# The second attention's exponentials in units of three heads instead of pairs

## The chip, the cores and the metric

The kernel runs on one core of one Trainium2 chip. The metric is the device time of one execution in microseconds; a kernel's time is the median over its runs. The core has four computing engines that run their own instruction streams and meet at semaphores: TensorE (PE in the profile, with PEld for its weight loads), VectorE (DVE), ScalarE (ACT) and GpSimd (POOL). SyncE (SP) issues the transfers. TensorE writes its results into eight banks of PSUM, each 512 fp32 columns wide on 128 partitions; ScalarE and VectorE read them there and write SBUF.

## The reference, cut to what matters

Two post-norm transformer layers over x of shape (4, 2048, 256), each an attention and a feed-forward part. Only the second layer's attention is touched:

```python
H, HD = 16, 16
q, k, v = (x @ Wq.T, x @ Wk.T, x @ Wv.T)      # reshaped to (B, S, H, HD)
q, k = _rope(q, k)
scores = jnp.einsum('bqhd,bkhd->bhqk', q, k) / np.sqrt(HD)
scores = jnp.where(causal, -jnp.inf, scores)
attn = jax.nn.softmax(scores, axis=-1)
out = jnp.einsum('bhqk,bkhd->bqhd', attn, v).reshape(B, S, 256)
return out @ Wo.T
```

## The kernel before

The program is a sequence of phases: set-up, projections of layer 0, its attention, its feed-forward part, then the same for layer 1. `attend_phase(nc, kn, layer)` builds both attentions; the branches with `layer == 1` are the second one.

**Tiling.** Scores are computed transposed, 128 keys on the partitions by 512 queries (TG) in the columns, one PSUM bank for one head. Four heads (HQ) are worked on together. A *step* S is one such tile for four heads; on the diagonal `even_steps` puts two pieces of narrower width side by side, so that every step is 512 columns wide. A set is one batch and one quad of heads: 34 steps (NST), in four query groups with 2, 7, 10 and 15 steps in order of their arrival. There are 16 sets, so N = 544 steps and 2176 heads of scores.

**Per step in the second attention.** PE multiplies keys by queries (L739, bf16, one matmul of 512 columns per head, two or more narrower ones on diagonal steps) into banks 0 to 5. ScalarE takes the exponential (L805) from PSUM into `prob`, a ring of R = 4 steps in SBUF. On masked steps VectorE sets entries above the diagonal to zero with a minimum (L844, `diagonal`). PE multiplies `prob` by the values, with a column of ones for the sum (L768, `weigh`; fp32, two matmul records per head in the profile, the four heads in four strips of 32 rows of one bank), adding up over the steps of a query group in bank 6 or 7. At the end of a group VectorE transposes, divides and transposes again (`normalise`), and SP stores.

**Pairs.** Scores are made by `scores(S, pair)`, two heads at a time, into one of three pairs of banks. The pair's index is 2S + pair. Before it writes, PE waits for exponential number 2S + pair - 3 (L731), the last reader of these banks. ScalarE runs 1088 exponentials of two heads, 1024 columns each; each waits for its scores (`qk`) and for the weighing of step S - 4, whose place in `prob` it overwrites (`pv`, L804).

**Order on PE.** It is written out by hand. In the second attention each turn S of the loop at L773 issues `scores(S + 1, 0)`, `weigh(S - 2)`, `scores(S + 1, 1)`. Between two weighings thus stand the second pair of one step and the first pair of the next.

**Order elsewhere.** ScalarE goes through the pairs in order. VectorE masks step S where it must and then does the normalising that is due, which waits for the weighing (`pv`) of the group's last step. SP loads *stacks* (keys, queries, values of one query group, 14 transfers each); queries are in a ring of three (QU), so the load of group n waits for the first transpose of group n - 3 (`o_tr`). PE waits for a stack at the group's first step (L729).

`Count` numbers the events of one semaphore; `c.wait(eng, n)` returns once event n has happened, and for a negative n at once.

Of the kernel before, what the change touches and what calls it, by code (L numbers as in the profile page):

```python
# [20 lines left out]
ACT = mybir.ActivationFunctionType  # L21
# [4 lines left out]
H, HD = 16, 16  # L26
P = 128
DC = D // P
TG = 512
GB = T // TG  # L30
TT = TG // P
KB = T // P
CB = TG // P
HQ = 4
# [590 lines left out]
def attend_phase(nc, kn, layer):  # L625
# [9 lines left out]
    N = N_SET * NST  # L635
    NG = N_SET * GB
    ND = sum(1 for _, m in steps if m)
    R = 4
    LAG = 2
    QU, KU = 3, 6  # L640
    QK0, E0, O0 = 0, 4, 6
    SR, FR = (QROWS, FROWS + 3) if layer == 0 else (QROWS + 3, 0)
    with ExitStack() as ctx:
# [3 lines left out]
        qk = ph.count("qk")  # L647
# [71 lines left out]
        @block.tensor  # L719
        def _(pe):  # L720
            for c in (qk, ex, pv):
                c.start(pe)
            pe.wait_ge(ones_in, 16)

            def scores(S, pair):
                it, _, pieces, _ = at(S)
                if pieces[0][1] == 0 and pair == 0:
                    n = it * GB + pieces[0][0]
                    pe.wait_ge(stacks_in[n % QU], (n // QU + 1) * (16 * N_LOAD))  # L729
                if layer == 1:  # L730
                    pr.wait(pe, 2 * S + pair - 3)  # L731
                elif pair == 0:
                    th.wait(pe, S - 1)
                for h in (2 * pair, 2 * pair + 1):
                    bank = QK0 + (h if layer == 0 else 2 * ((2 * S + pair) % 3) + h % 2)
                    for g, kb, q0, col, w in pieces:
                        n, c = it * GB + g, it * GB + kb // CB
                        keys = k_s[:, c % KU, h, (kb % CB) * P:(kb % CB + 1) * P]
                        mm = pe.matmul(ps[:, bank, col:col + w], keys, q_s[:, n % QU, h, q0:q0 + w], start=True, stop=True)  # L739
                if layer == 1 or pair == 1:  # L740
                    qk.done(mm)

            def extra(S, h):
                it, _, pieces, masked = at(S)

                sc.wait(pe, S * HQ + h - 2)
                for g, kb, q0, col, w in pieces:
                    n, c = it * GB + g, it * GB + kb // CB
                    mm = pe.matmul(ps[:, E0 + h % 2, col:col + w], g_s[:, c % KU, (kb % CB) * P:(kb % CB + 1) * P], f_s[:, n % QU, h, q0:q0 + w], start=True, stop=not masked)  # L749
                    if masked:  # L750
                        mm = pe.matmul(ps[:, E0 + h % 2, col:col + P], kn["identb"][:], kn["mask_kq"][:], start=False, stop=True)  # L751
                ex.done(mm)

            def weigh(S):
                it, s, pieces, masked = at(S)
                if layer == 0:
                    pr.wait(pe, S)
                elif masked:
                    kept.wait(pe, (it * ND + kept_at[s]) * 2 + 1)
                else:  # L760
                    pr.wait(pe, S * 2 + 1)
                for g, kb, q0, col, w in pieces:
                    n, c = it * GB + g, it * GB + kb // CB
                    if kb == 0:

                        o_tr.wait(pe, n - 2)
                    for h in range(HQ):
                        mm = pe.matmul(ps[VW * h:VW * (h + 1), O0 + n % 2, q0:q0 + w], v_s[:, c % KU, kb % CB, h * VW:(h + 1) * VW], prob[:, S % R, h, col:col + w], start=kb == 0, stop=g in ends[s] and (g, kb) == [p[:2] for p in pieces if p[0] == g][-1])  # L768
                pv.done(mm)

            scores(0, 0)
            scores(0, 1)
            for S in range(N + LAG):  # L773
                if layer == 1 and S + 1 < N:
                    scores(S + 1, 0)
                if S >= LAG:
                    weigh(S - LAG)
                if layer == 0 and S < N:
                    extra(S, 0)
                    extra(S, 1)  # L780
                    if S + 1 < N:
                        scores(S + 1, 0)
                if S + 1 < N:
                    scores(S + 1, 1)
                if layer == 0 and S < N:
                    extra(S, 2)
                    extra(S, 3)

        @block.scalar
        def _(act):  # L790
            for c in (th, pr):
                c.start(act)

            for S in range(N + 1):
                if S < N:
                    if layer == 0:
                        qk.wait(act, S)
                        sc.wait(act, (S - 2) * HQ + HQ - 1)
                        th.done(act.activation(tanh_s[:, S % 2], ps[:, QK0:QK0 + HQ], ACT.Tanh, scale=kn["rbeta"][:, 0:1]))  # L799
                    else:  # L800
                        for pair in range(2):
                            qk.wait(act, S * 2 + pair)
                            bank = QK0 + 2 * ((2 * S + pair) % 3)
                            pv.wait(act, S - R)  # L804
                            pr.done(act.activation(prob[:, S % R, 2 * pair:2 * pair + 2], ps[:, bank:bank + 2], ACT.Exp, scale=float(HD) ** -0.5))  # L805
                if S > 0 and layer == 0:
                    sc.wait(act, (S - 1) * HQ + HQ - 1)
                    pr.done(act.activation(prob[:, (S - 1) % R], prob[:, (S - 1) % R], ACT.Exp))  # L808

        @block.vector  # L810
        def _(dve):
            for c in (sc, o_tr, o_rc, o_mul, o_n, kept):
                c.start(dve)
            dve.memset(oq_s[:], 0.0).then_inc(padded, 1)
            dve.wait_ge(padded, 1)

            def normalise(due, count):

                for S, G, part in due[:count]:
                    v = G % 2  # L820
                    if part == 0:
                        pv.wait(dve, S)
                        o_mul.wait(dve, G - 2)
                        o_tr.done(dve.transpose(ot_s[:, v].rearrange("p b n -> p (b n)"), ps[:, O0 + v]))  # L824
                    elif part == 1:
                        o_tr.wait(dve, G)
                        o_rc.done(dve.reciprocal(rc_s[:, v], ot_s[:, v, :, HD]))
                    elif part == 2:
                        o_rc.wait(dve, G)
                        o_n.wait(dve, G - 2)  # L830
                        o_mul.done(dve.tensor_tensor(oq_s[:, v, :, 0:HD], ot_s[:, v, :, 0:HD], rc_s[:, v].unsqueeze(2).to_broadcast([P, NTB, HD]), ALU.mult))
                    else:
                        o_mul.wait(dve, G)
                        o_out.wait(dve, v, G // 2 - 1)
                        o_n.done(dve.transpose(on_s[:, v], oq_s[:, v].rearrange("p b n -> p (b n)")))
                del due[:count]

            def diagonal(S):

                masked = at(S)[3]  # L840
                for pair in range(2):
                    pr.wait(dve, S * 2 + pair)
                    block = blocks(prob[:, S % R, 2 * pair:2 * pair + 2], masked)
                    kept.done(dve.tensor_tensor(block, block, kn["keep"][:].unsqueeze(1).unsqueeze(1).to_broadcast([P, 2, len(masked), P]), ALU.min))  # L844

            def sums(S, due):

                pv.wait(dve, S - R)
                for h in range(HQ):
                    if h == 2:  # L850

                        normalise(due, 1)
                    th.wait(dve, S)
                    ex.wait(dve, S * HQ + h)
                    sc.done(dve.scalar_tensor_tensor(prob[:, S % R, h], tanh_s[:, S % 2, h], kn["alpha"][:, 0:1],  # L855
                                                     ps[:, E0 + h % 2], ALU.mult, ALU.add))

            due = []
            for S in range(N + LAG + 1):
                if S > LAG:  # L860
                    it, s, *_ = at(S - LAG - 1)
                    due += [(S - LAG - 1, it * GB + g, part) for g in ends[s] for part in range(4)]
                if S < N and layer == 0:
                    sums(S, due)
                else:
                    if S < N and at(S)[3]:
                        diagonal(S)
                    normalise(due, len(due))
            assert not due
# [711 lines left out]
```

## Time and profile before

| | |
|---|---|
| median of 3 runs | 4268.65 us (4263.97 to 4272.33) |
| profiled execution | 4269.56 us, span 4267.4 us |
| PE, PEld busy | 3718.8 us (87%), 1427.9 us (33%) |
| ACT, DVE busy | 3382.7 us (79%), 2744.3 us (64%) |
| second attention | first exponential at 2864.5 us, last at 3946.3 us |
| its exponentials (L805) | 1088, 1054.9 us busy, mean 1021 ns |
| mean granted TensorE clock | 0.968 of full speed |

The page gives the busy time of each engine as a share of the whole span, and the whole span has six stages with different limits. The stage to read is the second attention, about 1083 us from its first exponential to the end of its last. Two engines are nearly always busy in it. The rows further down cut the span by stretch, by line and in order of time. Names in rows: `ps` is PSUM, `att_q`, `att_k`, `att_v` and `att_prob` are the phase's tiles, `att_v<-v_ones` is the last transfer of a stack, and numbers like 128x1024 are partitions by columns. PE's records overlap, because a matmul is recorded until its last result has left the array, so the start of one to the start of the next is what a matmul costs.

### The profile page before, as it was taken

How to read it: one execution, taken by the hardware profiler on the slowest of the kernel's cores; microseconds unless marked ns; L12 is line 12 of the kernel's file. 1: busy time of each engine (PE TensorE's matmuls, PEld its weight loads, DVE VectorE, ACT ScalarE, POOL GpSimd, SP SyncE). 2: the span in 40 equal slices, each digit the busy share in tenths (PEclk: the TensorE clock that was granted, in tenths of full speed). 3: DMA queues.
4: the chain of work that ended last, by engine and by line, in shares of the span. 5: the costliest groups of instructions: out<-in, count | busy, mean ns of one | idle time of the engine just before them, and what ended most of it. 6: DMA issues, size and time to landing. Idle time of an engine off the chain costs nothing. (4 is left out here: it accounts for less than half of the span.)

```text
span 4267.4 us, 65356 instructions
## 1 busy us (share of the span) xinstructions
PE 3718.8 (87%) x21966; PEld 1427.9 (33%) x21966; DVE 2744.3 (64%) x4748; ACT 3382.7 (79%) x2760; POOL 450.1 (11%) x407
## 2 busy tenths in 40 slices
PE   6968989998998998899897857749999999999787
PEld 2422323222332322233232644422222222222565
DVE  5637887778888777888876978853323233232688
ACT  2428999999999999999998113339999999999233
POOL 3530000000000000000000216630000000000232
PEclk9979999999999999999999989879999999999899
DMA  5862111112111111211111545652222222221333
GB/s 168 260 200 57 52 53 45 46 50 60 52 53 52 45 45 51 60 51 54 52 45 45 147 146 159 195 149 69 71 76 72 65 79 68 76 73 48 110 89 89
DMA packets 307803, 360.37 MB, mean 84 GB/s; under 512 B 56590, under 2 KB 237934, under 8 KB 307249
## 3 DMA queue, kind: packets, MB, share of 16 engines
q1 hardware_dynamic: 307508, 356.62, 28.9%
q8 instruction: 163, 2.67, 0.3%
q14 instruction: 132, 1.08, 0.1%
HBM read 228.15 MB, written 128.25 MB: 84 GB/s over the span
## 5 line engine op out<-in xcount | busy, mean ns | idle before, releaser
L855 DVE SCALAR_TENSOR_TENSOR att_prob<-att_tanh,alpha,ps 128x512 f32<-128x512 f32 x2176 | 1507.2, 741 | 431.0 <-ACT att_tanh L799 371.1
L739 PE MATMUL ps<-att_q,att_k 99*128 99x512 bf16 (+5 forms) x5120 | 1136.7, 351 | 159.9 <-DMA att_v<-v_ones 104.0
L768 PE MATMUL ps<-att_prob,att_v 128*32 128x512 f32 (+3 forms) x10240 | 1161.8, 539 | 2.2 <-ACT att_prob L808 2.2
L799 ACT ACTIVATE att_tanh<-ps,rbeta 128x2048 f32<-128x2048 f32 x544 | 1110.6, 2042 | 59.8 <-PE ps L739 59.7
L805 ACT ACTIVATE att_prob<-ps 128x1024 f32<-128x1024 f32 x1088 | 1054.9, 1021 | 38.7 <-PE ps L739 22.9
L808 ACT ACTIVATE att_prob<-att_prob 128x2048 f32<-128x2048 f32 x544 | 1081.2, 1988 | 1.7 <-DVE att_prob L855 1.3
L749 PE MATMUL ps<-att_f,att_g 75*128 75x512 bf16 (+3 forms) x2560 | 810.4, 354 | 131.3 <-DVE att_prob L855 121.2
L739 PEld LDWEIGHTS ps<-att_q,att_k 96*128 96x128 bf16 (+1 forms) x5120 | 399.9, 98 | 1007.7 <-ACT att_prob L805 424.8
L844 DVE TENSOR_TENSOR att_prob<-att_prob,keep 128x512 f32<-128x512 f32 (+1 forms) x320 | 187.5, 586 | 587.9 <-ACT att_prob L805 586.8
L749 PEld LDWEIGHTS ps<-att_f,att_g 75*128 75x128 bf16 x2560 | 231.9, 96 | 922.1 <-DVE att_prob L855 899.5
L768 PEld LDWEIGHTS ps<-att_prob,att_v 128*32 128x32 f32 x10240 | 216.0, 108 | 347.9 <-ACT att_prob L805 139.0
L1233 POOL TENSOR_TENSOR post_x1b<-post_x,post_bias 128x256 f32<-128x256 f32 x64 | 46.6, 757 | 2193.3 <-DVE post_x L1042 2193.3
L404 POOL TENSOR_TENSOR proj_parts<-proj_rem,proj_parts 128x512 bf16<-128x512 f32 (+2 forms) x176 | 224.7, 1279 | 136.9 <-DVE proj_parts L564 97.9
L1031 ACT ACTIVATE post_n_sd<-post_n_mv,eps 128x4 f32<-128x4 f32 x64 | 18.9, 295 | 249.7 <-DVE post_n_mv L1026 249.7
L751 PE MATMUL ps<-mask_kq,identb 128*128 128x128 bf16 x1024 | 211.1, 221 | 0.0
L824 DVE STREAM_TRANSPOSE att_ot<-ps 128x512 f32<-128x512 f32 x128 | 91.2, 712 | 185.1 <-PE ps L768 185.1
L1458 POOL TENSOR_SCALAR post_prev<-post_xt,post_om 128x512 f32<-128x512 f32 x64 | 56.8, 905 | 1188.9 <-issue 1146.4
L564 DVE CAST proj_parts<-proj_rem 128x512 bf16<-128x512 f32 (+2 forms) x176 | 152.6, 871 | 0.0
L421 ACT ACTIVATE proj_vs<-ps 128x512 f32<-128x512 f32 x64 | 38.2, 597 | 136.2 <-PE ps L516 96.8
L1042 DVE TENSOR_SCALAR post_x<-post_rr,post_n_rs,post_n_nb 128x256 f32<-128x256 f32 x256 | 122.1, 539 | 7.4 <-DVE post_n_nb L1037 0.2
L508 PE MATMUL ps<-proj_xt,proj_wq 128*128 128x512 f32 x256 | 125.7, 637 | 0.8 <-ACT proj_xt L430 0.8
L516 PE MATMUL ps<-proj_wv,proj_xt 128*128 128x256 f32 x512 | 123.5, 384 | 1.8 <-ACT proj_vs L421 1.5
(132 smaller groups left out, 2462.4 us busy)
## 6 DMA issues: line engine op xcount, KB each, us to landing
att_k<-k_parts SPq DMA_DIRECT2D x768, 64.0 KB
att_q<-q_parts SPq DMA_DIRECT2D x768, 64.0 KB
v_ones<-proj_vs SPq DMA_DIRECT2D x128, 256.0 KB, 3.1
att_v<-v_ones SPq DMA_DIRECT2D x128, 256.0 KB
post_o<-o_t SPq DMA_DIRECT2D x40, 512.0 KB, 5.1
att_f<-f_parts SPq DMA_DIRECT2D x384, 48.0 KB
o_t<-att_on SPq DMA_DIRECT2D x512, 32.0 KB, 1.9
q_parts<-proj_parts SPq DMA_DIRECT2D x32, 384.0 KB, 4.2
```

What stands on the lines that cost most here:

```text
L404: low.done(pool.tensor_tensor(parts[0:n, rp, 2], rem[0:n, r], parts[0:n, rp, 1], ALU.subtract))
L508: mm = pe.matmul(ps[0:n, PRJ0 + r], lhs, xt[:, u, c], start=c == 0, stop=c == DC - 1)
L564: mid.done(dve.tensor_copy(parts[0:n, (s - L_MID) % RP, 1], rem[0:n, r]))
L739: mm = pe.matmul(ps[:, bank, col:col + w], keys, q_s[:, n % QU, h, q0:q0 + w], start=True, stop=True)
L749: mm = pe.matmul(ps[:, E0 + h % 2, col:col + w], g_s[:, c % KU, (kb % CB) * P:(kb % CB + 1) * P], f_s[:, n % QU, h, q0:q0 + w], start=True ...
L751: mm = pe.matmul(ps[:, E0 + h % 2, col:col + P], kn["identb"][:], kn["mask_kq"][:], start=False, stop=True)
L768: mm = pe.matmul(ps[VW * h:VW * (h + 1), O0 + n % 2, q0:q0 + w], v_s[:, c % KU, kb % CB, h * VW:(h + 1) * VW], prob[:, S % R, h, col:col + ...
L799: th.done(act.activation(tanh_s[:, S % 2], ps[:, QK0:QK0 + HQ], ACT.Tanh, scale=kn["rbeta"][:, 0:1]))
L805: pr.done(act.activation(prob[:, S % R, 2 * pair:2 * pair + 2], ps[:, bank:bank + 2], ACT.Exp, scale=float(HD) ** -0.5))
L808: pr.done(act.activation(prob[:, (S - 1) % R], prob[:, (S - 1) % R], ACT.Exp))
L844: kept.done(dve.tensor_tensor(block, block, kn["keep"][:].unsqueeze(1).unsqueeze(1).to_broadcast([P, 2, len(masked), P]), ALU.min))
L855: sc.done(dve.scalar_tensor_tensor(prob[:, S % R, h], tanh_s[:, S % 2, h], kn["alpha"][:, 0:1], ps[:, E0 + h % 2], ALU.mult, ALU.add))
```

## The change

In the second attention the heads of all steps form one stream, numbered 4S + h. A *unit* is three heads of this stream. There are 726 units, of which the last has one head. Unit u writes banks 0 to 2 or 3 to 5 in turn, waits for exponential u - 2, and is read by one exponential of 1536 columns, which writes three neighbouring places in `prob`, now a ring of six steps. A step's last head lies in unit (4S + 3) // 3; the weighing of the step is issued after the unit three further on. Units cross the borders of steps, groups and sets. The masks wait for the unit that holds their heads. In the first attention the issue order stays: its two pairs of scores were already next to each other. The code of both is separated.

```diff
-    R = 4
+    R = 4 if layer == 0 else 6
...
+    UH = 3
+    NU = -(-N * HQ // UH)
...
+            def score(S, h, bank):
                 it, _, pieces, _ = at(S)
-                if pieces[0][1] == 0 and pair == 0:
+                if pieces[0][1] == 0 and h == 0:
                     n = it * GB + pieces[0][0]
                     pe.wait_ge(stacks_in[n % QU], (n // QU + 1) * (16 * N_LOAD))
-                if layer == 1:
-                    pr.wait(pe, 2 * S + pair - 3)
-                elif pair == 0:
+                for g, kb, q0, col, w in pieces:
+                    n, c = it * GB + g, it * GB + kb // CB
+                    keys = k_s[:, c % KU, h, (kb % CB) * P:(kb % CB + 1) * P]
+                    mm = pe.matmul(ps[:, bank, col:col + w], keys, q_s[:, n % QU, h, q0:q0 + w], start=True, stop=True)
+                return mm
...
+            def unit(u):
+
+                pr.wait(pe, u - 2)
+                for i in range(UH * u, min(UH * (u + 1), N * HQ)):
+                    mm = score(i // HQ, i % HQ, QK0 + i % (2 * UH))
+                qk.done(mm)
...
-                    pr.wait(pe, S * 2 + 1)
+                    pr.wait(pe, (S * HQ + HQ - 1) // UH)
...
+            if layer == 1:
+                w = 0
+                for u in range(NU + UH):
+                    if u < NU:
+                        unit(u)
+                    while w < N and (w * HQ + HQ - 1) // UH <= u - UH:
+                        weigh(w)
+                        w += 1
+                assert w == N
...
+            if layer == 1:
+                slots = prob[:].rearrange("p r h t -> p (r h) t")
+                for u in range(NU):
+                    i, n = UH * u, min(UH, N * HQ - UH * u)
+                    qk.wait(act, u)
+                    pv.wait(act, (i + n - 1) // HQ - R)
+                    pr.done(act.activation(slots[:, i % (R * HQ):i % (R * HQ) + n], ps[:, QK0 + i % (2 * UH):QK0 + i % (2 * UH) + n], ACT.Exp, scale=float(HD) ** -0.5))
...
-                    pr.wait(dve, S * 2 + pair)
+                    pr.wait(dve, (S * HQ + 2 * pair + 1) // UH)
```

The order on PE at the start of the second attention, where `att_q` and `att_k` are the factors of the scores and `att_prob` and `att_v` those of the weighing; x4 of 512 columns is four heads. Before:

```order
L739 MATMUL ps<-att_q,att_k 128x512 x4
L739 MATMUL ps<-att_q,att_k 128x256 x4
L768 MATMUL ps<-att_prob,att_v 32x512 x4
L739 MATMUL ps<-att_q,att_k 128x256 x4
L739 MATMUL ps<-att_q,att_k 128x512 x2
L768 MATMUL ps<-att_prob,att_v 32x128 x4
```

and after, at the same place (L735 are the scores, L779 the weighing):

```order
L735 MATMUL ps<-att_q,att_k 128x512 x4
L735 MATMUL ps<-att_q,att_k 128x256 x6
L779 MATMUL ps<-att_prob,att_v 32x512 x4
L735 MATMUL ps<-att_q,att_k 128x256 x2
L735 MATMUL ps<-att_q,att_k 128x512 x2
L779 MATMUL ps<-att_prob,att_v 32x128 x4
```

One more head of scores (two matmuls of 256 columns) now stands before the first weighing.

The same engine in the middle of a later set, where plain steps meet diagonal ones. Before:

```order
L739 MATMUL ps<-att_q,att_k 128x512 x4
L768 MATMUL ps<-att_prob,att_v 32x512 x4
L739 MATMUL ps<-att_q,att_k 128x512 x2
L739 MATMUL ps<-att_q,att_k 128x128
L739 MATMUL ps<-att_q,att_k 128x384
L739 MATMUL ps<-att_q,att_k 128x128
L739 MATMUL ps<-att_q,att_k 128x384
L768 MATMUL ps<-att_prob,att_v 32x512 x4
```

and after:

```order
L735 MATMUL ps<-att_q,att_k 128x512 x3
L779 MATMUL ps<-att_prob,att_v 32x512 x4
L735 MATMUL ps<-att_q,att_k 128x512 x6
L779 MATMUL ps<-att_prob,att_v 32x512 x4
L735 MATMUL ps<-att_q,att_k 128x512
L735 MATMUL ps<-att_q,att_k 128x128
L735 MATMUL ps<-att_q,att_k 128x384
L735 MATMUL ps<-att_q,att_k 128x128
L735 MATMUL ps<-att_q,att_k 128x384
L779 MATMUL ps<-att_prob,att_v 32x512 x4
```

The blocks of scores between weighings went from four heads each to three, three and six in turn; no two weighings became neighbours here.

On ScalarE the phase's 1088 exponentials of 128x1024 (L805) became 725 of 128x1536 and one of 128x512 (L817).

## Rows read from the trace of the kernel before

**Rows 1.** Busy time by stretch; the header names the columns:

```profile
core 0: us, PE busy (x) PEld busy (x) DVE busy (x) ACT busy (x) POOL busy (x), PEclk, DMA share, GB/s
2863.00:2877.00 14.00, 8.18 (x29) 2.82 (x30) 2.88 (x5) 6.63 (x7) 0.00 (x0) 0.50 0.42 114
2895.00:3947.00 1052.00, 1048.03 (x7490) 297.81 (x7494) 308.44 (x554) 1031.12 (x1064) 0.00 (x0) 1.00 0.25 70
...
3072.20:3205.90 133.70, 133.70 (x968) 38.27 (x960) 40.12 (x72) 131.66 (x137) 0.00 (x0) 1.00 0.26 73
```

**Rows 2.** Groups by shape, 3072.5 to 3205.5 us; the first row names the columns:

```profile
line engine op names shapes xcount | busy us, mean ns | idle before us <-releasers
L805 ACT ACTIVATE att_prob<-ps 128x1024 f32<-128x1024 f32 x136 | 131.9, 1021 | 2.0
L739 PE MATMUL ps<-att_q,att_k 99*128 99x512 bf16 x224 | 60.0, 382 | 0.0
L768 PE MATMUL ps<-att_prob,att_v 128*32 128x512 f32 x448 | 59.8, 605 | 0.0
L739 PEld LDWEIGHTS ps<-att_q,att_k 99*128 99x128 bf16 x320 | 24.8, 97 | 68.6 <-ACT att_prob L805 53.6
...
L844 DVE TENSOR_TENSOR att_prob<-att_prob,keep 128x512 f32<-128x512 f32 x24 | 16.6, 693 | 12.8 <-ACT att_prob L805 12.7
```

**Rows 3.** The timeline, 3200 to 3212 us; columns in its first row:

```profile
start us, us, engine line op out<-in xcount [idle before <-releaser]
3200.51 1.04 PE L739 MATMUL ps<-att_q,att_k 99*128 99x512 bf16 x4
3201.48 1.06 PE L768 MATMUL ps<-att_prob,att_v 128*32 128x512 f32 x8
...
3202.48 1.04 PE L739 MATMUL ps<-att_q,att_k 99*128 99x512 bf16 x6
```

**Rows 4.** Two single lines; count: duration ns min/median/max, first and last start, forms:

```profile
L805 ACT ACTIVATE att_prob<-ps x136: 1017/1021/1024, 3072.2 to 3205.1; 128x1024 f32<-128x1024 f32 x136
...
L739 PE MATMUL ps<-att_q,att_k x320: 219/379/391, 3072.6 to 3205.1; 99*128 99x512 bf16 x112, 99*128 99x128 bf16 x32, 99*128 99x256 bf16 x16
```

**Rows 5.** The timeline of ScalarE alone, at four moments:

```profile
3200.11 1.02 ACT L805 ACTIVATE att_prob<-ps 128x1024 f32<-128x1024 f32 x1
...
3201.16 1.02 ACT L805 ACTIVATE att_prob<-ps 128x1024 f32<-128x1024 f32 x1
...
3202.08 1.02 ACT L805 ACTIVATE att_prob<-ps 128x1024 f32<-128x1024 f32 x1
...
3203.12 1.02 ACT L805 ACTIVATE att_prob<-ps 128x1024 f32<-128x1024 f32 x1
```

**Rows 6.** Who waited for whom, 2860 to 3950 us:

```profile
PEld ps L739 <- ACT att_prob L805: 424.8, 538, 1.7
...
PE ps L739 <- DMA att_v<-v_ones: 41.1, 11, 31.7
```

**Rows 7.** ScalarE's groups by shape, whole run:

```profile
L799 ACT ACTIVATE att_tanh<-ps,rbeta 128x2048 f32<-128x2048 f32 x544 | 1110.6, 2042 | 59.8 <-PE ps L739 59.7
...
L421 ACT ACTIVATE proj_vs<-ps 128x512 f32<-128x512 f32 x64 | 38.2, 597 | 136.2 <-PE ps L516 96.8 <-DMA v_ones<-proj_vs 39.4
```

**Rows 8.** The timeline of the first attention, a release of PE by ScalarE:

```profile
1200.92 2.09 ACT L799 ACTIVATE att_tanh<-ps,rbeta 128x2048 f32<-128x2048 f32 x1
...
1203.06 0.11 PEld L739 LDWEIGHTS ps<-att_q,att_k 96*128 96x128 bf16 x2 [0.33 <-ACT att_tanh L799]
```

**Rows 9.** The timeline where the second attention starts:

```profile
2872.39 2.74 PE L739 MATMUL ps<-att_q,att_k 99*128 99x512 bf16 x8 [5.41 <-DMA att_v<-v_ones]
...
2873.47 2.85 ACT L805 ACTIVATE att_prob<-ps 128x1024 f32<-128x1024 f32 x3 [5.23 <-PE ps L739]
...
2875.07 1.94 PE L768 MATMUL ps<-att_prob,att_v 128*32 128x512 f32 x8
...
2876.93 1.31 PE L739 MATMUL ps<-att_q,att_k 99*128 99x256 bf16 x6
```

More of the change, by code:

```diff
@@ L723, in _, with scores @@
             pe.wait_ge(ones_in, 16)
-            def scores(S, pair):
+            def score(S, h, bank):
                 it, _, pieces, _ = at(S)
-                if pieces[0][1] == 0 and pair == 0:
+                if pieces[0][1] == 0 and h == 0:
                     n = it * GB + pieces[0][0]
                     pe.wait_ge(stacks_in[n % QU], (n // QU + 1) * (16 * N_LOAD))
-                if layer == 1:
-                    pr.wait(pe, 2 * S + pair - 3)
-                elif pair == 0:
+                for g, kb, q0, col, w in pieces:
[3 more added lines that the diff above has]
+                return mm
+            def scores(S, pair):
+                if pair == 0:
                     th.wait(pe, S - 1)
                 for h in (2 * pair, 2 * pair + 1):
[L735 to L740, printed above, removed]
-                    qk.done(mm)
+                    mm = score(S, h, QK0 + h)
+                if pair == 1:
+                    qk.done(mm)
+            def unit(u):
[3 more added lines that the diff above has]
+                qk.done(mm)
             def extra(S, h):
@@ L769, in weigh @@
                 pv.done(mm)
[L771 to L787, printed above, removed]
+            if layer == 1:
[7 more added lines that the diff above has]
+                assert w == N
+            else:
+                scores(0, 0)
+                scores(0, 1)
+                for S in range(N + LAG):
+                    if S >= LAG:
+                        weigh(S - LAG)
+                    if S < N:
+                        extra(S, 0)
+                        extra(S, 1)
+                        if S + 1 < N:
+                            scores(S + 1, 0)
+                            scores(S + 1, 1)
+                        extra(S, 2)
+                        extra(S, 3)
         @block.scalar
@@ L792, in _ @@
                 c.start(act)
-            for S in range(N + 1):
-                if S < N:
-                    if layer == 0:
+            if layer == 1:
[5 more added lines that the diff above has]
+                    pr.done(act.activation(slots[:, i % (R * HQ):i % (R * HQ) + n], ps[:, QK0 + i % (2 * UH):QK0 + i % (2 * UH) + n], ACT.Exp, scale=float(HD) ** -0.5))
+            else:
+                for S in range(N + 1):
+                    if S < N:
                         qk.wait(act, S)
@@ L799, in _ @@
                         th.done(act.activation(tanh_s[:, S % 2], ps[:, QK0:QK0 + HQ], ACT.Tanh, scale=kn["rbeta"][:, 0:1]))
[L800 to L808, printed above, removed]
+                    if S > 0:
+                        sc.wait(act, (S - 1) * HQ + HQ - 1)
+                        pr.done(act.activation(prob[:, (S - 1) % R], prob[:, (S - 1) % R], ACT.Exp))
         @block.vector
```

## Prediction

> **What bounds the kernel now.** I first read the busy time by stretch, to see whether one engine fills the second attention and at which clock [rows 1]. From 2895 to 3947 us TensorE is busy 1048.03 of 1052.00 us at a granted clock of 1.00, ScalarE 1031.12. Both look full, and a share of busy time can't say which one sets the pace. So I next took a stretch without a transfer wait and looked at the idle time in front of each group [rows 2]: in it no PE group has any idle time before it (0.0), while the exponentials have 2.0 us before 136 of them. Then the order of time [rows 3]: the reader is to see that PE alternates without a break, a block of four score matmuls at 3200.51, a weighing at 3201.48, the next block at 3202.48. That is 0.97 + 1.00 = 1.97 us for a step of four heads. The same beat holds over the 136 exponentials from 3072.2 to 3205.1 [rows 4]: 132.9 / 135 x 2 = 1.97.
>
> ScalarE follows this beat. Its exponentials of two heads last 1.02 us and start at 3200.11, 3201.16, 3202.08, 3203.12 [rows 5]: alternately 1.05 or 1.04 and 0.92 apart. At 0.92 the second begins before the first has ended; at 1.05 it came after a gap, waiting for scores. ScalarE alone would need 2 x 0.92 = 1.84 per step and has 1.97. What the waits call "PEld waits for ACT" (424.8 us) [rows 6] is the idle weight loader, not the array: its loads are 0.10 us each [rows 2] and lie under matmuls.
>
> I therefore read the second attention as bound by TensorE with ScalarE 7% behind, and this decides the forecast.
>
> **Part 1: 725 exponentials of three heads and one of one head for 1088 of two.** One head of 512 columns takes 0.597 us, two take 1.021 [rows 7, 2], so a third adds 0.42 and three take 1.45; where they queue they start 0.10 less apart, 1.35. Four of them for three steps: 5.39, against 6 x 0.92 = 5.52 before. ScalarE's own work falls by 0.13 x 181 = 24 us. But three steps of PE last 3 x 1.97 = 5.90, so this gain falls wholly into ScalarE's idle time: 0 on the path. Bounds of the three-head time: 1.44 from below by the rows just used; from above three quarters of the 2.04 that four banks take in the tanh, 1.53 [rows 7]. I take 1.45, since the two-bank row has the same function, the same operands and the nearest size. The Trainium skill (ScalarE: Activation LUTs, What ACT_TABLE_LOAD costs) gives 186 ns + 0.833 ns per column for immediate scale and bias, 1.47 for three heads; its 1.04 for two is a little over the trace's 1.02, and with it the margins below would be 0.02 smaller.
>
> **Part 2: what PE does is the same.** The order shows the same 2176 heads of scores and 544 weighings. A weighing still stands alone between blocks of scores; only the blocks are 3, 3 and 6 heads in place of 4, 4, 4. A score matmul costs 0.22: a block of four lasts 1.04, whose last record is 0.38, and (1.04 - 0.38) / 3 = 0.22 [rows 3, 4]. Turning from scores to weighing costs 0.97 - 4 x 0.22 = 0.09, a weighing with the turn back 1.00. Three steps after: 12 x 0.22 + 3 x 0.09 + 3 x 1.00 = 5.91, which is three steps before. Cost 0, if no wait binds.
>
> **Part 3: the ring of scores.** Before, pair k waited for exponential k - 3, and one pair was always spare. Now unit u waits for exponential u - 2. Put unit 4 at 0 (units run 4, W, 5, W, 6, W, 7, 8, W..., W a weighing). PE: unit 4 at 0, W 0.74, unit 5 1.74, W 2.48, unit 6 3.49, W 4.24, unit 7 5.25, unit 8 5.90. An exponential can start 0.65 after its pair's block began (3200.51 to 3201.16 [rows 3, 5]), so 0.87 after a unit of three did. Exponential 3 runs 0.20 to 1.65, 4 from 1.55 to 3.00, 5 from 2.90 to 4.34, 6 waits for its scores and runs 4.36 to 5.81. PE starts 0.05 after the end of the activation it waits for (2.09 from 1200.92, load at 1203.06) [rows 8]. So unit 5 may start at 1.70 and does at 1.74; unit 8 may at 5.86 and does at 5.90; units 6 and 7 have 0.45 and more. Two of four waits are met with only 0.04 us to spare. In one sentence, from unit 6 to unit 8: PE's own chain is 0.66 + 0.09 + 1.00 + 0.66 = 2.41, the chain over ScalarE 0.87 + 1.45 + 0.05 = 2.37. One thing does reach PE: at unit 8 the weight load can't be pulled far ahead. A block's first matmul after such a load is recorded at up to 0.391 against a median of 0.379 [rows 4], so I take 0.01 x 181 = 2 us. Bounds: 0, and the whole 0.10 of a load [rows 2] less the 0.04 to spare, 11 us.
>
> **Part 4: masks and ring of six.** In one step of three both masks now wait for the same exponential; two of 0.69 [rows 2], with as much as PE's 0.05 of release before each, end 1.5 after it, and that step's weighing starts at 4.24, 2.6 after exponential 3 ended. Cover is left, cost 0; the same for the two others, where the first half is ready earlier. If the cover went, a weighing would be late by the rest of 0.7. The exponential waits for the weighing six steps back, which is long done; with four steps it would stand at the limit, so the deeper ring pays for the skew and costs nothing on the path. SP's loads are released by the transposes behind the last weighing of a group. Between that weighing and the first score that needs the third stack lie 26 heads and six weighings now, and 25, 26 or 27 heads and six after. PE's waits for stacks, 41.1 - 31.7 = 9.4 us over ten sets [rows 6], thus stay on the mean: 0, with 1 us either way.
>
> **Part 5: the start.** Before, heads 0 to 7 are scored, PE is idle for 5.41 until the second stack is there at 2872.39, and three more pairs (the eight matmuls of that row) go before the first weighing at 2875.07 [rows 9]. After, unit 2 holds heads 6, 7 and 8, so its exponential waits for the stack too: head 8 takes twice 0.22 at half clock, the exponential runs from about 2873.05 (0.2 behind the score, as the one at 2873.47 was behind its two) to 2874.5, while unit 3 is scored by 2874.1. Unit 4 waits 0.5, and one more head (0.2 to 0.4, as the granted clock there is 0.50 [rows 1], the lower level of 1.2 GHz) goes before the first weighing. Cost about 0.7, from 0 to 2.5: the upper end is one weighing at half clock, 1.86 for 1.00 [rows 9], if the pause delays the rise of the clock. At the end the last weighings follow each other as before: 0.
>
> **Sum.** 0.7 + 2 = 2.7 us on the profiled execution's 4269.56: 4272.3. The median of the runs, 4268.65, is 0.9 below that execution, so the forecast is 4271. A difference of 0.2%, 8.5 us, is about what can be told from no change.
>
> **Rival A, slower: the chain over two units becomes the bound.** Place: unit 6, its exponential, unit 8. It decides once exponential plus release last over 1.54 (now 1.45 + 0.05). With 1.53 for three banks the deficit is 0.87 + 1.53 + 0.05 - 2.41 = 0.04, 8 us; with the load exposed, 11 us; with both whole, 0.14 x 181 = 25 us. Time 4277 to 4294, in the middle 4285. For it: where three pairs of banks took turns there are now two units, and the margin is 0.04. Against: the sizes come from like rows, and the two narrow places follow each other without adding. Chance 0.20.
>
> **Rival B, faster: ScalarE is the bound after all**, as PE's records overlap and its busy time proves little. Then a step would go from 1.97 to 5.39 / 3 = 1.80, and 544 x 0.17 = 92 us would be gained: 4176. Even without the smaller fixed cost a step would fall to the 1.84 of today's pairs. The Trainium skill (Perfetto Trace Analysis, Identifying the Most-Contended Engine) says that matmul busy time is a poor measure and that the share of weight loads is the better one; here that share is 38.27 of 133.70 us, 29% [rows 1], which would speak for this rival. Against it speak the starts: blocks at a constant 1.97, nothing idle before PE, and gaps on ScalarE. Chance 0.08.
>
> **Rival C: the compiled order doesn't hold the three-head form.** The order shows 725 of 1536 columns and one of 512, so 0.02, at no change.
>
> **How the numbers follow.** Forecast case 0.70, from 4264 (runs scatter by 4 below) to 4277. A 0.20, of which 0.03 stays within 0.2%; B 0.08; C 0.02. Faster 0.08, same 0.75, slower 0.17. The range from 4262 to 4287 takes the forecast case, C and two thirds of A, 0.85; its upper end is the middle of A with 2 us of scatter.
>
> **What would show it.** PE's blocks starting 5.90 apart per three steps, no ACT release before unit 8, and exponentials of 1.45 with some 0.3 us of idle before the one behind a weighing: right. A PE gap before every fourth unit: rival A, and its size the deficit. Steps near 1.80: rival B. Third-stack waits much over 0.9 us would break part 4, a first weighing later than 2877 part 5. The forecast is wrong if a three-head exponential lasts over 1.50, or if the turn between scores and weighings turns out to be a wait.

## The result and the profile after

The changed kernel takes 4285.94 us in the median (4282.43 to 4289.19, 6 runs), the kernel before 4269.1 in the runs beside it (4263.97 to 4272.91, 6 runs). The ratio is 1.0041, 95% interval 1.0030 to 1.0051: it is 0.3 to 0.5% slower, 17 us. The forecast was 4271 in a range from 4262 to 4287, with 0.75 for no change (within 0.2%) and 0.17 for slower. The range holds the time, but near its upper end; the likeliest case was the wrong one.

The page of the changed kernel, its span and the busy times by engine:

```profile
span 4283.5 us, 64582 instructions
## 1 busy us (share of the span) xinstructions
PE 3716.1 (87%) x21958; PEld 1416.7 (33%) x21966; DVE 2736.6 (64%) x4748; ACT 3342.4 (78%) x2398; POOL 450.1 (11%) x407
```

ScalarE's busy time fell from 3382.7 to 3342.4 us and the span grew from 4267.4 to 4283.5. Now the line view of the exponentials over the whole run (duration min/median/max, then first and last start), to be held against the first and last start in the table of the kernel before:

```profile
engine op xcount: duration ns min/median/max, first and last start us, forms
L817 ACT ACTIVATE att_prob<-ps x726: 607/1451/1460, 2866.6 to 3961.7; 128x1536 f32<-128x1536 f32 x182
```

From the first to the last start are 3961.7 - 2866.6 = 1095.1 us; before it was 3946.3 - 2864.5 = 1081.8. So 13.3 of the 16.1 us that the span grew lie inside the second attention. The rest is 2.1 in front (0.4 of it the third head, before which the first exponential can't start) and 0.7 behind. The code there is the same, and in the eight experiments below the first exponential starts anywhere between 2867.1 and 2872.8, so these few us are not put down to the change.

The stretch of [rows 2] again, groups by shape with the idle time before them, after:

```profile
line engine op names shapes xcount | busy us, mean ns | idle before us <-releasers
L817 ACT ACTIVATE att_prob<-ps 128x1536 f32<-128x1536 f32 x90 | 125.9, 1451 | 8.0 <-PE ps L735 7.6
L779 PE MATMUL ps<-att_prob,att_v 128*32 128x512 f32 x444 | 59.2, 605 | 0.0
L735 PE MATMUL ps<-att_q,att_k 99*128 99x512 bf16 x220 | 59.2, 382 | 0.9 <-DMA att_v<-v_ones 0.9
```

The three-head exponential takes 1.451 us, as forecast. PE still has almost no idle time before its groups; the 0.9 is a wait for a transfer. The timeline in the middle of this stage, the rows that answer to [rows 3]:

```profile
start us, us, engine line op out<-in xcount [idle before <-releaser]
...
3063.54 1.47 PE L735 MATMUL ps<-att_q,att_k 99*128 99x512 bf16 x6
3064.15 0.36 PEld L735 LDWEIGHTS ps<-att_q,att_k 99*128 99x128 bf16 x3 [0.28 <-ACT att_prob L817]
3064.40 4.13 ACT L817 ACTIVATE att_prob<-ps 128x1536 f32<-128x1536 f32 x3 [0.30 <-PE ps L735]
...
3064.94 1.07 PE L779 MATMUL ps<-att_prob,att_v 128*32 128x512 f32 x8
...
3065.94 0.82 PE L735 MATMUL ps<-att_q,att_k 99*128 99x512 bf16 x3
...
3066.69 1.06 PE L779 MATMUL ps<-att_prob,att_v 128*32 128x512 f32 x8
```

Six scores start at 3063.54, the weighing at 3064.94, the next unit at 3065.94. This is the beat of part 3: 0.65 + 0.65 + 0.10, then 1.00, then 0.75 to the weighing at 3066.69. The row at 3064.15 is unit 8's weight load. It is released by an exponential and comes about 0.05 ahead of 3064.19, when the three scores before it (0.65) are through. Four starts of ScalarE, as in [rows 5]:

```profile
3062.65 1.45 ACT L817 ACTIVATE att_prob<-ps 128x1536 f32<-128x1536 f32 x1
...
3064.40 1.45 ACT L817 ACTIVATE att_prob<-ps 128x1536 f32<-128x1536 f32 x1 [0.30 <-PE ps L735]
...
3065.75 1.45 ACT L817 ACTIVATE att_prob<-ps 128x1536 f32<-128x1536 f32 x1
...
3067.08 1.46 ACT L817 ACTIVATE att_prob<-ps 128x1536 f32<-128x1536 f32 x1
```

1.75, 1.35 and 1.33 apart: two exponentials begin before the one ahead has ended, one waited for its scores. That is the pattern that was forecast. What has grown is found in the list of waits, the rows that answer to [rows 6] (total, times, longest):

```profile
ACT att_prob L817 <- PE ps L735: 89.4, 210, 11.3
PE ps L735 <- DMA att_v<-v_ones: 50.5, 16, 31.4
...
PE ps L735 <- ACT att_prob L817: 2.0, 3, 1.5
```

PE's waits for the last transfer of a stack are 50.5 us in 16 against 41.1 in 11. Each list holds the wait for the first stack (31.4 and 31.7) and the one for the second at the start (4.77 and 5.41), so the waits inside the stage are 14.3 us in 14 places against 4.0 in nine. To the 14 belongs a fifteenth, which the list puts down to an exponential, the 1.5 in its last row:

```profile
3908.45 0.36 SPq L698 DMA_DIRECT2D att_v<-v_ones  x1
...
3911.58 0.81 PE L735 MATMUL ps<-att_q,att_k 99*128 99x512 bf16 x3 [1.51 <-ACT att_prob L817]
```

The exponential that happened to end at 3911.56 is that of the unit just before, and this unit waits for the one before that, which ended at 3909.80. The place is the third stack of the last set, and the last transfer of this stack was issued at 3908.45, 3.13 us before the score could start; at 3842.98, the border shown below, it was 2.88. So 15.8 us in 15 places stand against 4.0 in nine, and PE truly waits for an exponential only twice, 0.26 us each, in the first ten microseconds of the stage. (The recorded expectations below put the stack waits inside the stage at 17.6; the rows give 15.8.)

### Where the transfer wait comes from

The border between two sets, before. The first row is the last weighing of a set (16 records, 1.07 us), then come masks and the first transpose on VectorE, the issue of the loads that the transpose releases, and the score that needs their stack:

```profile
3815.45 1.07 PE L768 MATMUL ps<-att_prob,att_v 128*32 128x128 f32 x16
3816.18 0.69 DVE L844 TENSOR_TENSOR att_prob<-att_prob,keep 128x512 f32<-128x512 f32 x1 [0.37 <-ACT att_prob L805]
...
3816.79 0.71 DVE L824 STREAM_TRANSPOSE att_ot<-ps 128x512 f32<-128x512 f32 x1
...
3817.59 4.10 SPq L597 DMA_DIRECT2D att_k<-k_parts  x6
...
3829.14 0.60 PE L739 MATMUL ps<-att_q,att_k 99*128 99x512 bf16 x2 [0.26 <-DMA att_v<-v_ones]
```

The weighing ends at 3816.52, the transpose starts at 3816.79, the loads are issued from 3817.59, PE waits 0.26 for them at the score of 3829.14. The same border of the changed kernel:

```profile
3827.96 1.07 PE L779 MATMUL ps<-att_prob,att_v 128*32 128x128 f32 x16
...
3829.83 0.69 DVE L862 TENSOR_TENSOR att_prob<-att_prob,keep 128x512 f32<-128x512 f32 x1 [0.65 <-ACT att_prob L817]
...
3830.44 0.71 DVE L842 STREAM_TRANSPOSE att_ot<-ps 128x512 f32<-128x512 f32 x1
...
3831.24 4.53 SPq L597 DMA_DIRECT2D att_k<-k_parts  x6
...
3842.98 0.39 PE L735 MATMUL ps<-att_q,att_k 99*128 99x512 bf16 x1 [1.58 <-DMA att_v<-v_ones]
```

The weighing ends at 3829.03, the transpose starts at 3830.44, 1.41 behind it in place of 0.27, and PE waits 1.58. In front of the transpose on VectorE's queue stands the second mask of the next set's second step (3829.83). It waited 0.65 for its exponential, which with three heads is later than the pair's was. Before, this mask began at 3816.18, ahead of the weighing's end, and held the transpose up by 0.2 at most: in e1 below, with no mask in front, the transpose starts 0.07 behind the weighing. At the 15 borders the transpose follows the weighing by 1.08 to 1.41 us after the change, and always by 0.27 before. The waits scatter more than this, from 0.32 to 1.77, so the way from the transpose to the landed stack varies too (issuing the six loads of the fourth row took 4.53 here and 4.10 before); why it does was not looked into.

### The profile page after: what moved, and what is told of

The parts are those of the page before. It is cut to its first block and busy times, and to the rows that moved or that the text cites. A ratio compares the mean times of both kernels' runs of the same rounds, so it can differ in the third digit from the quotient of the medians.

```text
span 4283.5 us, 64582 instructions
## 1 busy us (share of the span) xinstructions
PE 3716.1 (87%) x21958; PEld 1416.7 (33%) x21966; DVE 2736.6 (64%) x4748; ACT 3342.4 (78%) x2398; POOL 450.1 (11%) x407
## 5 line engine op out<-in xcount | busy, mean ns | idle before, releaser
L735 PE MATMUL ps<-att_q,att_k 99*128 99x512 bf16 (+5 forms) x5120 | 1138.9, 351 | 171.8 <-DMA att_v<-v_ones 115.1
L779 PE MATMUL ps<-att_prob,att_v 128*32 128x512 f32 (+3 forms) x10240 | 1162.2, 540 | 2.5 <-ACT att_prob L826 2.2
L817 ACT ACTIVATE att_prob<-ps 128x1536 f32<-128x1536 f32 x726 | 1014.5, 1450 | 92.5 <-PE ps L735 89.4
L735 PEld LDWEIGHTS ps<-att_q,att_k 96*128 96x128 bf16 (+1 forms) x5120 | 392.4, 98 | 1030.6 <-ACT att_prob L817 403.9
L779 PEld LDWEIGHTS ps<-att_prob,att_v 128*32 128x32 f32 x10240 | 216.4, 108 | 345.5 <-issue 196.6
```

The costliest lines, as they stand in the source:

```text
L817: pr.done(act.activation(slots[:, i % (R * HQ):i % (R * HQ) + n], ps[:, QK0 + i % (2 * UH):QK0 + i % (2 * UH) + n], ACT.Exp, scale=float(H ...
```

## Experiments

Eight kernels were run. e1 to e4 were measured beside the kernel before at 4271.84 us, e5 to e8 beside the same kernel at 4273.23, so times across the two groups can differ by a microsecond or two for that alone. Two theories stood against each other. **Q:** the loss is PE's wait for the third stack of a set, because the transpose that releases the load is queued behind a mask that now comes later. **R:** the ring of two units is too tight and holds PE up (rival A of the prediction).

**e1, the transpose ahead of the masks.** The changed kernel, in VectorE's loop:

```diff
+                elif S < N and at(S)[3] and S >= 2 and ends[at(S - 2)[1]]:
+                    it, s, *_ = at(S - 2)
+                    ahead = [(S - 2, it * GB + g, 0) for g in ends[s]]
+                    early.update(x[:2] for x in ahead)
+                    normalise(ahead, len(ahead))
+                    diagonal(S)
+                    normalise(due, len(due))
```

> The changed kernel with one thing moved on VectorE: at the end of a set the first transpose goes ahead of the masks of the next set's second step. Theory Q (the loss is PE's wait for the third stack of a set, because the transpose that releases its load is queued on VectorE behind a mask that now waits for a later, longer exponential): the transpose starts 0.3 us after the last weighing's end in place of 1.1 to 1.4, the stack waits of 15 sets fall from 17.6 us in sum to about 5, and the time from 4286 to about 4273 (4271 to 4276). Theory R (the ring of two units holds PE up): nothing changes, 4284 to 4288.

Measured: 4274.08 us against 4271.84 of the kernel before beside it, ratio 1.0005 (0.9996 to 1.0014), where the changed kernel had 1.0041. One border and the list of waits:

```profile
3824.02 1.07 PE L779 MATMUL ps<-att_prob,att_v 128*32 128x128 f32 x16
...
3825.16 0.72 DVE L842 STREAM_TRANSPOSE att_ot<-ps 128x512 f32<-128x512 f32 x1 [1.20 <-PE ps L779]
...
3825.80 1.25 DVE L862 TENSOR_TENSOR att_prob<-att_prob,keep 128x512 f32<-128x512 f32 x2
...
3838.00 0.39 PE L735 MATMUL ps<-att_q,att_k 99*128 99x512 bf16 x1 [0.55 <-DMA att_v<-v_ones]
```

```profile
PE ps L735 <- DMA att_v<-v_ones: 39.6, 9, 31.7
```

The weighing ends at 3825.09 and the transpose starts at 3825.16; the masks follow at 3825.80. Nine waits are left, 39.6 in all; less the two of the start (31.7 and 4.6) that is 3.3 in seven places, as in the kernel before with its 4.0 in nine. Only the place of one VectorE instruction per set differs from the changed kernel, so Q holds and R doesn't explain the loss.

**e2, the same delay in the kernel before.** A memset between the wait for a set's last weighing and the transpose:

```diff
                         pv.wait(dve, S)
+                        if layer == 1 and G % GB == GB - 1:
+                            dve.memset(late[:], 0.0)
```

> The kernel before with a filler of about 0.9 us on VectorE between the wait for the last weighing of a set and the transpose behind it; scores, exponentials and ring stay as they were. Theory Q: PE waits about 0.6 to 0.9 us longer in each of 15 sets, 9 to 13 us in all, near 4280. Theory R: the filler lies in VectorE's idle time and costs nothing, 4267 to 4271.

Measured: 4287.58 us against 4271.84, ratio 1.0035 (1.0021 to 1.0049). A border, then the waits:

```profile
3080.82 1.07 PE L769 MATMUL ps<-att_prob,att_v 128*32 128x128 f32 x16
...
3082.40 0.91 DVE L825 MEMSET att_late<- 128x1024 f32 x1 [0.16 <-issue]
3083.23 0.65 DVE L827 STREAM_TRANSPOSE att_ot<-ps 128x512 f32<-128x512 f32 x1
...
3083.97 3.67 SPq L597 DMA_DIRECT2D att_k<-k_parts  x6
...
3094.96 0.39 PE L740 MATMUL ps<-att_q,att_k 99*128 99x512 bf16 x1 [0.72 <-DMA att_v<-v_ones]
```

```profile
PE ps L740 <- DMA att_v<-v_ones: 51.0, 17, 31.4
```

The weighing ends at 3081.89, the transpose starts 1.34 later behind 0.91 us of filler. With scores, exponentials and ring as they were, the kernel loses as much as by the change. The waits are 51.0 in 17, or 14.4 in 15 without the two of the start, nearly those of the changed kernel. The time is 16 us above the kernel before where 9 to 13 were expected; in the profiled execution the stage takes 1093.4 us from first to last exponential (2867.1 to 3960.5), 11.6 more than before, which is within what was expected.

**e3 and e4, room for one more stack.** In the changed kernel and in the one before:

```diff
-    QU, KU = 3, 6
+    QU, KU = (3, 6) if layer == 0 else (4, 8)
```

> The changed kernel with room for four stacks of queries and eight of keys and values in the second attention in place of three and six, so that a load is released one group earlier. Theory Q: all waits for third stacks go, 17.6 us, and the time is about 4268 (4266 to 4271), the start's 0.5 us being the rest. Theory R: 4284 to 4288.

> The kernel before with the same four and eight places. Theory Q: its 5 us of waits for third stacks go, about 4264 (4262 to 4266), and it stands within 5 us of the changed kernel with the same room. Theory R: 4264 too, but 17 to 22 us below the changed kernel with the same room.

Measured: e3 4269.6, ratio 0.9992 (0.9983 to 1.0001); e4 4265.83, ratio 0.9986 (0.9977 to 0.9995). PE's waits for stacks, e3 and then e4, and the line view of their exponentials:

```profile
PE ps L735 <- DMA att_v<-v_ones: 35.9, 2, 31.3
...
PE ps L739 <- DMA att_v<-v_ones: 36.7, 2, 31.6
```

```profile
L817 ACT ACTIVATE att_prob<-ps x726: 607/1451/1460, 2870.8 to 3948.7; 128x1536 f32<-128x1536 f32 x182
...
L805 ACT ACTIVATE att_prob<-ps x1088: 1017/1023/1045, 2867.2 to 3943.5; 128x1024 f32<-128x1024 f32 x182
```

Two waits are left in each, those of the start. The stage lasts 3948.7 - 2870.8 = 1077.9 us with units of three and 3943.5 - 2867.2 = 1076.3 with pairs. So the stack waits cost the changed kernel 17.2 us (1095.1 - 1077.9) and the kernel before 5.5. The difference of the two, 11.7, agrees with the 15.8 - 4.0 = 11.8 read from the waits. All else that the change does to the stage costs 1.6 together, and of this the start takes 0.9 (see part 5 below). With units and pairs on equal terms, R is worth at most a microsecond. In the medians e3 lies 3.8 us above e4; in the profiled executions the rest of that stands mainly in front of the first exponential (2870.8 against 2867.2), where the code is the same. Of the versions that compute the whole result, e4 is the only one that is faster than the kernel before by more than its interval, by 0.1%.

**e5 and e6, is TensorE the bound?** e4 and e3 with the fourth head's score left out from the seventh step on; its exponential reads what lies in the bank.

```diff
+                    if layer == 1 and h == 3 and S >= 6:
+                        continue
```

> The kernel before with four and eight stacks; from step 6 of the second attention on, the fourth head's score matmul is left out (its exponential reads what lies in the bank), so PE has 0.22 us less per step and ScalarE the same work. If TensorE sets the step's 1.97 us, it falls to what ScalarE alone needs, 2 x 0.92 = 1.84: 538 x 0.13 = 70 us, 4266 to 4196. If ScalarE or a wait between the two set it, the time stays at 4266.

> The changed kernel with four and eight stacks, and the fourth head's score left out in the same way. With TensorE out of the way the three-head exponentials should show what they save: 5.39 us per three steps against 5.52, so 24 us below the kernel before with the same cut, about 4173 to 4180. If the two units are too tight a ring for it, the gain is not reached: 4190 to 4215, at or above the kernel before with the same cut.

Measured: e5 4194.75, ratio 0.9816 (0.9799 to 0.9832); e6 4195.29, 0.9816 (0.9800 to 0.9833). Their exponentials, e5 first:

```profile
L807 ACT ACTIVATE att_prob<-ps x1088: 1017/1643/1652, 2870.7 to 3873.5; 128x1024 f32<-128x1024 f32 x182
...
L819 ACT ACTIVATE att_prob<-ps x726: 605/1451/1511, 2871.0 to 3875.2; 128x1536 f32<-128x1536 f32 x182
```

Taking 0.22 us per step from PE, and nothing from ScalarE, makes the kernel before 71 us faster. The stage goes from 1076.3 to 1002.8 us, which is 1.84 per step, what ScalarE needs for its pairs. This shows that TensorE set the step. (A chain that runs through both engines would have become shorter as well; against it stands that no group of PE's had idle time before it in [rows 2], and e7 below tests it from the other side.) e6 is no faster than e5: the 24 us by which its exponentials are cheaper don't appear. The stage of 1004.2 us over 544 steps is 1.85 per step against the 1.80 of queued exponentials of three heads. So two units don't give back what the longer exponentials save, even with TensorE relieved. The trace of e6 shows the place, unit 8 of part 3:

```profile
3178.82 1.55 PE L735 MATMUL ps<-att_q,att_k 99*128 99x512 bf16 x5
...
3179.54 0.33 PEld L735 LDWEIGHTS ps<-att_q,att_k 99*128 99x128 bf16 x3 [0.61 <-ACT att_prob L819]
```

Unit 7, here of two heads, starts at 3178.82, and unit 8 has to wait for exponential 6; its load goes at 3179.54. From there PE has no break until the next unit 7, whose scores come too late for ScalarE: over the middle of the stage, the exponentials start 1.35, 1.33, 1.33 and 1.53 apart in the median, and in the mean 5.50 per three steps, where four queued ones need 5.39. The pairs of e5 take 5.50 as well.

The exponentials of e5 are recorded with 1.643 us though they start 0.92 apart, so there the record is longer than the cost.

**e7 and e8, how much room is there?** e4 and e3 with a longer exponential: the scale, the same value, is read from a column.

```diff
-ACT.Exp, scale=float(HD) ** -0.5
+ACT.Exp, scale=kn["rbeta"][:, 0:1]
```

> The kernel before with four and eight stacks; the exponentials take their scale, the same 0.25, from a column in SBUF, which lengthens each by some 0.05 to 0.09 us. Per step 1.94 to 2.02 us of ScalarE against TensorE's 1.97: 0 to 28 us, 4266 to 4294.

> The changed kernel with four and eight stacks and the same longer exponentials, now one per three heads. The chain from a unit over its exponential to the unit after next, 2.37, grows to 2.42 to 2.46 against TensorE's 2.41: if the margin is the 0.04 us of the prediction, 2 to 9 us, 4272 to 4279. If there is far more room, 4270.

Measured: e7 4289.79, ratio 1.0038 (1.0024 to 1.0053); e8 4287.05, 1.0031 (1.0018 to 1.0043). Their exponentials:

```profile
L805 ACT ACTIVATE att_prob<-ps,rbeta x1088: 1106/1772/1795, 2867.3 to 3966.5; 128x1024 f32<-128x1024 f32 x182
...
L817 ACT ACTIVATE att_prob<-ps,rbeta x726: 689/1542/1554, 2868.5 to 3963.2; 128x1536 f32<-128x1536 f32 x182
```

The three-head exponential grew by 0.09 (1.451 to 1.542) and the stage by 16.8 us, 1094.7 against 1077.9, or 0.093 per three steps. That is a miss: 2 to 9 us were expected, from 0.87 + 1.54 + 0.05 - 2.41 = 0.05 for the narrow place at most. Its trace shows where the rest comes from:

```profile
3176.82 2.97 ACT L817 ACTIVATE att_prob<-ps,rbeta 128x1536 f32<-128x1536 f32 x2
...
3179.08 1.59 PE L735 MATMUL ps<-att_q,att_k 99*128 99x512 bf16 x6
...
3179.84 0.33 PEld L735 LDWEIGHTS ps<-att_q,att_k 99*128 99x128 bf16 x3 [0.43 <-ACT att_prob L817]
```

Exponentials 5 and 6 run without a break from 3176.82 to 3179.79, unit 7 starts at 3179.08, and unit 8's load comes 0.76 behind it, where it came 0.61 behind in the changed kernel. Over the middle of the stage (units 60 to 699) unit 8 starts 0.748 after unit 7 in the mean, in e3 0.659; the other three distances stay at 1.74 to 1.75. So one narrow place takes the whole loss, and the other, unit 5, still doesn't wait. The 0.87 of the sum is what failed: exponential 6 now queues behind exponential 5 and starts 0.895 after its unit, in e3 0.860. 0.895 + 1.55 + 0.055 = 2.50 is 0.09 more than 2.41. In e3 unit 8 starts 0.098 after the end of exponential 6 and in e8, where it waits, 0.055: the room was 0.04, as forecast. e7's stage takes 1099.2, 22.9 more than e4's: two longer exponentials per step come to 2.02 a step, which makes ScalarE the bound there. ScalarE's work grew by 0.18 per step (from 2 x 0.92 to 2 x 1.01) and the step by 22.9 / 544 = 0.04, so about 0.14 fell into idle time, which again puts TensorE ahead by the 0.13 of the prediction.

## Why the prediction was right and wrong

- **The bound.** Right: TensorE sets the step, ScalarE has 0.13 us to spare. e5 shows it by its 71 us, e7 by the 0.14 of 0.18 that cost nothing.
- **Part 1, cheaper exponentials.** Right: 1.451 us measured for 1.45, and the gain of 24 us falls into idle time. e6 adds that it wouldn't come out with the two units even if TensorE were faster, which the text didn't say.
- **Part 2, PE's own work.** Right: the beat of three steps is unchanged, 5.90 in the mean over the middle of the stage in e3 and in e4.
- **Part 3, the ring.** The mechanism and the margin were right (the load at 3064.15 with 0.05 to spare, the 0.04 of e8), and so was that the two narrow places don't add. The 2 us for late weight loads were too much: start and ring together come to the 1.6 us by which e3's stage is longer than e4's.
- **Part 4, the stack waits.** This is the step that failed. It set "0, with 1 us either way"; the runs show 17.2 - 5.5 = 11.7 us. Its own sign, third-stack waits much over 0.9 us, came in part: there are 15 waits of 1.05 in the mean, nine of them from 1.2 to 1.8, where there were nine of 0.44. The step compared only PE's distance from the last weighing to the score that needs the stack, which did stay the same, and took the way from the weighing over the transpose to the load as fixed. But on VectorE the masks of the next set's second step stand in front of this transpose. The same part did look at these masks, and asked only whether they would be late for their own weighing, which they are not. What is queued behind the mask was not asked. A smaller fault lies in the same term: the 9.4 us in "ten sets" held 5.41 of the second stack at the start; 4.0 us in nine sets would have been right, as the rows gave.
- **Part 5, the start.** Forecast 0.7 us. From the landing of the second stack to the first weighing the changed kernel takes 2877.43 - 2873.89 = 3.54 us against 2875.07 - 2872.39 = 2.68, which is 0.9 more, in keeping with the 1.6 for start and ring. The sign "a first weighing later than 2877" did come, by 0.4, because the stack itself landed 1.5 later. The clock rose no later: the granted clock is 0.52 in the 14 us from 2866 and 1.00 in the next 14, before 0.50 in the 14 us from 2863 and 0.98 in the next 14.
- **Rival A** gave 4277 to 4294, and the time fell there, but its place was another one: PE waited for an exponential twice, 0.5 us in all. The range reached up to 4287 because of this rival, which did not happen, and the time fell inside it by a cause that the prediction had put at nothing. That is luck.
- **Rival B** is out by e5: there ScalarE's work stayed as it was, and the time fell by 71 us. The rule that it leaned on (the Trainium skill, Perfetto Trace Analysis, Identifying the Most-Contended Engine) is that for TensorE the headroom is to be judged by the share of peak arithmetic and the busy share of weight loads, and not by the busy share of matmuls. The share of weight loads alone would have misled here: it was 29%, and PE was the bound. What told it was the distance from start to start.

## What to carry to other kernels

When an instruction comes later, go through the queue it stands in, and ask what stands behind it and whom that releases, also where its own result has time to spare. Here a mask that was on time for its reader delayed a transpose, the transpose a load, and the load TensorE: 11.7 us over 15 borders. Before making the second busiest engine's work cheaper, take work from the busiest and see that the time follows, as e5 does: if it follows, the busiest is the bound, and cheaper work on the other has nothing to give.

## What the runs showed of the hardware

An activation's scale taken from a column of SBUF in place of a constant makes the three-head exponential 0.09 us longer (1.451 to 1.542). The recorded length of an activation can be far over what it costs when activations stand one behind the other without a break: 1.643 in e5, with starts 0.92 apart, against 1.023 in e4, where every second one waits for its scores, with the same operands.
